# The last expert layer of a four-layer decoder: row scatters replaced by a slot table and gathers

## The reference

```python
group_scores = sg.max(axis=-1)
_, gtop = jax.lax.top_k(group_scores, LG)
keep_g = jnp.sum(jax.nn.one_hot(gtop, G, dtype=jnp.float32), axis=1) > 0
masked = jnp.where(keep_g[:, :, None], sg, -jnp.inf).reshape(-1, E)
_, idx = jax.lax.top_k(masked, K)
...
cap = max(1, int(CAP_FACTOR * N * K / E))
pos = (jnp.cumsum(oh, axis=0) * oh).sum(-1) - 1
keep = pos < cap
...
xe = xp[buf_tok].reshape(E, cap, DIM)
h = jax.nn.silu(jnp.einsum('ecd,edh->ech', xe, w1)) * jnp.einsum('ecd,edh->ech', xe, w3)
out = jnp.einsum('ech,ehd->ecd', h, w2) * buf_w.reshape(E, cap, 1)
y = jnp.zeros((N + 1, DIM), x.dtype).at[buf_tok].add(out.reshape(E * cap, DIM))[:N]
z = jax.nn.silu(xf @ sw1) * (xf @ sw3) @ sw2
return (y + z).reshape(shape)
```

## Time and profile before

| what | us |
|---|---|
| three runs, lowest / median / highest | 3349.03 / 3350.38 / 3354.73 |
| the profiled execution, its own time | 3352.86 |
| its span, first to last instruction | 3351.1 |
| PE busy (86% of the span) | 2880.7 |
| DVE busy (57%) | 1918.6 |
| ACT busy (42%) | 1409.0 |
| POOL busy (18%) | 598.1 |

### The profile page before, as it was taken

One profiled execution on the slowest core, in us unless ns is written; L12 is line 12 of the kernel. 1 busy time (PEld: TensorE's weight loads), 2 busy tenths in 40 slices (PEclk: granted clock), 3 DMA queues, 4 the chain that ended last, 5 costly groups with the idle time before them and its releaser, 6 DMA issues. The chain is left out here.

```text
span 3351.1 us, 46532 instructions
## 1 busy us (share of the span) xinstructions
PE 2880.7 (86%) x13948; PEld 2113.6 (63%) x13949; DVE 1918.6 (57%) x3700; ACT 1409.0 (42%) x2923; POOL 598.1 (18%) x544
## 2 busy tenths in 40 slices
PE   5695789965997989999599999999999997256997
PEld 4684455535885779999366666666666664234664
DVE  4314465405555354444688888888888884442332
ACT  1233534421211224445277676777767775100000
POOL 0122101111331200000201111111111111154554
PEclk9797879986998879999799999999999998587998
DMA  1342000003232010000011000001100000425776
GB/s 39 128 136 82 14 14 14 14 0 110 82 99 88 1 39 26 25 13 1 23 27 24 22 18 19 20 16 29 21 22 20 16 15 3 184 81 160 168 170 136
DMA packets 157228, 177.45 MB, mean 53 GB/s; under 512 B 37664, under 2 KB 130998, under 8 KB 155510
## 3 DMA queue, kind: packets, MB, share of 16 engines
q1 hardware_dynamic: 120150, 116.15, 12.1%
q0 software_dynamic: 20512, 35.54, 4.7%
q10 hardware_dynamic: 16416, 24.12, 2.1%
HBM read 105.77 MB, written 49.18 MB: 46 GB/s over the span
## 5 line engine op out<-in xcount | busy, mean ns | idle before, releaser
L2065 DVE TENSOR_TENSOR l3a_pt_lo<-l3a_pt,l3a_pt_hi 128x512 fp32r<-128x512 f32 (+2 forms) x640 | 463.8, 730 | 96.4 <-ACT l3a_pt L1959 92.1
L1958 ACT ACTIVATE l3a_pt_hi<-l3a_banks 128x512 fp32r<-128x512 f32 (+2 forms) x640 | 382.5, 598 | 322.7 <-PE l3a_banks L1904 258.8
L1959 ACT ACTIVATE l3a_pt<-l3a_banks 128x512 f32<-128x512 f32 (+2 forms) x640 | 378.0, 591 | 0.0
L2039 DVE TENSOR_REDUCE l3a_maxima<-l3a_banks 128x1 f32<-128x1178 f32 x256 | 351.1, 1375 | 1.8 <-PE l3a_banks L1855 0.6
L1904 PE MATMUL l3a_banks<-l3a_pt_hi,l3a_v 128*65 128x512 f32 (+2 forms) x640 | 286.6, 448 | 8.0 <-ACT l3a_out L1973 8.0
L1914 PE MATMUL l3a_banks<-l3a_q,l3a_k 128*128 128x512 f32 (+2 forms) x640 | 257.1, 402 | 7.4 <-DVE l3a_q L2002 4.6
L1915 PE MATMUL l3a_banks<-l3a_q,l3a_k 72*128 72x512 f32 (+5 forms) x640 | 253.8, 397 | 0.0
L1904 PE MATMUL l3a_banks<-l3a_pt_hi,l3a_v_lo 128*65 128x512 f32 (+2 forms) x640 | 252.7, 395 | 0.0
L1904 PE MATMUL l3a_banks<-l3a_pt_lo,l3a_v 128*65 128x512 f32 (+2 forms) x640 | 252.5, 394 | 0.0
L1855 PE MATMUL l3a_banks<-l3a_k,l3a_q 128*128 128x512 f32 (+1 forms) x768 | 213.1, 387 | 18.6 <-DVE l3a_maxima L2039 17.5
L1855 PEld LDWEIGHTS l3a_banks<-l3a_k,l3a_q 128*128 128x128 f32 x768 | 139.6, 192 | 64.0 <-DVE l3a_maxima L2039 41.9
(11 more groups left out here) (563 smaller groups left out, 6065.0 us busy)
## 6 DMA issues: line engine op xcount, KB each, us to landing
l3f_w<-in_L_ffn_w SPq DMA_DIRECT2D x96, 256.0 KB, 3.1
l0f_w<-in_L_ffn_W ACTq DMA_DIRECT2D x12, 1024.0 KB, 6.5
l3f_slots_x<-l3f_empty SPq DMA_DIRECT2D x10, 1168.0 KB, 15.4
l3f_x_rows<-l3f_slots_x SPq DMA_DIRECT2D x32, 292.0 KB, 3.9
l1f_w<-in_L_ffn_W ACTq DMA_DIRECT2D x18, 512.0 KB, 5.2
l2f_w<-in_L_ffn_w SPq DMA_DIRECT2D x16, 512.0 KB, 4.5
l3a_q<-l3a_q SPq DMA_DIRECT2D x64, 128.0 KB, 2.3
l3a_k<-l3a_k SPq DMA_DIRECT2D x64, 128.0 KB, 2.3
```

Source lines behind the costliest of these rows:

```text
L1958: act.activation(a.pt_hi[0:rows, n % a.pt_slots, :], a.st_bank[0:rows, n % 2, :], ACT.Exp, bias=bias, scale=scale)
L1959: act.activation(a.pt[0:rows, n % 4, :], a.st_bank[0:rows, n % 2, :], ACT.Exp, bias=bias, scale=scale).then_inc(a.exped, 1)
L2039: dve.tensor_reduce(a.maxima[:, n:n + 1], banks.rearrange("p a b -> p (a b)")[:, 0:KEYS], AX.X, ALU.max).then_inc(a.maxed, 1)
L2065: dve.tensor_tensor(a.pt_lo[0:rows, slot, :], a.pt[0:rows, n % 4, :], a.pt_hi[0:rows, slot, :].bitcast(F32), ALU.subtract).then_inc(a.lo_m ...
```

## The change

The expert picks use an operation that returns the eight largest values of a row (`max`) and one that replaces given values in a row (`match_replace`), once per tile. A slot number, one over all experts (384 slots each), is split into lane (lowest seven bits) and column (the rest, 96 of them). One-hot rows of column times token number and of lane, multiplied on PE and summed over the 64 (tile, pick) pairs, give a table: lane x column to token. POOL gathers each expert's rows with it from one copy of the rows in DRAM. The shared expert's blocks move in between.

```diff
-            for n in range(CLEARS):
-                rows = slots_x[n * P * CLEAR:(n + 1) * P * CLEAR, :].rearrange("(p n) d -> p (n d)", p=P)
-                sp.dma_start(rows, empty[:].rearrange("p n d -> p (n d)")).then_inc(cleared, 16)
...
+            for q in range(4):
+                sp.dma_start(rows[4 * q * P:4 * (q + 1) * P, :].rearrange("(t p) d -> p t d", p=P), x_ext[:, 4 * q:4 * (q + 1), :]
+                             ).then_inc(rows_kept, 16)
...
-                    load_rows(sp, e + 2, u)
...
-                for t in range(TILES):
-                    pool.indirect_dma_start(slots_x, bass.IndirectOffsetOnAxis(scatter_index[:, k, t:t + 1], 0), x_ext[:, t, :], None
-                                            ).then_inc(scattered, 16)
+            def fetch(u):
+                for j, (at, n) in enumerate(PIECES):
+                    pool.indirect_dma_start(x_rows[0:n, u, j, :], None, rows, bass.IndirectOffsetOnAxis(in_index[0:n, u, j:j + 1], 0)
+                                            ).then_inc(x_loaded[u], 16)
...
+            def run(e, u, more, first=False):
+                if more:
+                    pool.wait_ge(indexed, e + 1)
+                    pool.sem_inc(taken, 1)
+                    fetch(u)
+                if not first:
+                    pool.wait_ge(summed, e * 48)
+                    pool.sem_inc(y_free, 1)
                 pool.wait_ge(meta_kept, e + 1)
                 pool.wait_ge(y_kept, e * 3 + 4)
...
-                pool.wait_ge(summed, e * 48 + 48)
-                pool.sem_inc(y_free, 1)
...
+            shared_hidden(2)
+            for n in range(ENTRIES):
...
+                ins = pe.matmul(p_y[:, 0, 0:TABLE], at_lane[:, n, :], of_token[:, n, :], start=n == 0, stop=n == ENTRIES - 1)
+            ins.then_inc(inverted, 1)
...
+            def take_largest(largest, values, width, left):
+                for t in range(TILES):
+                    ins = dve.max(largest[:, t, :], values[:, t, 0:width])
+                step(ins)
+                step(dve.memset(largest[:, :, K:8], NEVER))
+                for t in range(TILES):
+                    ins = dve.match_replace(left[:, t, :], largest[:, t, :], values[:, t, :], TAKEN)
+                step(ins)
```

More of the change, by code:

```diff
@@ L2823, in run @@
                                             compute_op=ALU.add).then_inc(summed, 16)
-                pool.wait_ge(summed, e * 48 + 48)
-                pool.sem_inc(y_free, 1)
-            experts(pool, run)
+            run(0, 0, True, first=True)
+            run(1, 1, True)
+            with pool.Fori(1, E // 2 - 1) as i:
+                for u in range(2):
+                    run(i * 2 + u, u, True)
+            for u in range(2):
+                run(E - 2 + u, u, False)
         @block.tensor
@@ L2918, in _, with shared_silu @@
             act.copy(probs[:], scores[:]).then_inc(probs_kept, 1)
-            for b in range(4):
+            def shared_silu(b):
                 for f in range(FC):
@@ L2950, in _ @@
             dve.wait_ge(probs_kept, 1)
-            dve.wait_ge(constants, 5)
+            dve.wait_ge(constants, 10)
             step(dve.tensor_scalar(restart[:], restart[:], 0.0, None, ALU.is_gt))
-            step(dve.tensor_reduce(groups[:].rearrange("p t g -> p (t g)"), scores[:].rearrange("p t (g n) -> p (t g) n", g=G), AX.X, ALU.max))
-            for k in range(KEPT_GROUPS):
-                choose(dve, step, groups[:], group_pick[:], group_order[:], total[:], best[:], 2.0)
-            step(dve.tensor_scalar(group_kept[:], groups[:], 0.0, 2.0, ALU.is_ge, ALU.mult))
@@ new lines, in shared_mult, with shared_add @@
+            def shared_mult(b):
+                for f in range(FC):
+                    dve.wait_ge(z_silu_kept, b * FC + f + 1)
+                    if b >= 1:
+                        dve.wait_ge(z_out, 4 * b)
+                    dve.tensor_tensor(z_hidden[:, f, :], z_silu[:, f, :], p_h[:, 2 + f, :], ALU.mult).then_inc(z_kept, 1)
+            def shared_add(b):
+                for t in range(4 * b, 4 * b + 4):
+                    dve.wait_ge(z_out, t + 1)
+                    dve.scalar_tensor_tensor(chip.x[:, t, :], p_xt[:, t % 2, 0:D], chip.gates[:, 7:8], chip.x[:, t, :],
+                                             ALU.mult, ALU.add).then_inc(z_added, 1)
@@ L2966, in _ @@
+            shared_mult(0)
+            take_largest(largest_scores, open_scores, E, left_scores)
+            shared_add(0)
+            step(dve.tensor_scalar(chosen[:], left_scores[:, :, 0:E], TAKEN, None, ALU.is_le))
             dve.sem_inc(chose, 1)
-            step(dve.tensor_reduce(total[:], weight[:].rearrange("p k t -> p t k"), AX.X, ALU.add))
+            step(dve.tensor_reduce(total[:], largest_scores[:, :, 0:K], AX.X, ALU.add))
             step(dve.tensor_scalar(total[:], total[:], 1e-9, None, ALU.add))
@@ L2990, in _ @@
[L2990 to L2999 removed]
+            step(dve.tensor_tensor(scores[:], chosen[:], rank[:].rearrange("p e t -> p t e"), ALU.mult))
@@ new lines, in _ @@
+            for t in range(TILES):
+                ins = dve.max(places[:, t, :], scores[:, t, :])
+            step(ins)
+            step(dve.tensor_scalar(slot[:], places[:, :, 0:K], -1.0, None, ALU.add))
+            step(dve.tensor_scalar(lane[:], slot[:], P - 1, None, ALU.bitwise_and))
+            step(dve.tensor_scalar(column_of[:], slot[:], 7, None, ALU.logical_shift_right))
+            shared_mult(1)
+            flat_lane, flat_column = lane[:].rearrange("p t k -> p (t k)"), column_of[:].rearrange("p t k -> p (t k)")
@@ new lines, in _ @@
+            shared_mult(2)
+            dve.wait_ge(inverted, 1)
+            step(dve.scalar_tensor_tensor(spare[:], p_y[:, 0, 0:TABLE], 0.0, own[:], ALU.is_equal, ALU.mult))
+            step(dve.scalar_tensor_tensor(table[:, 0:TABLE], p_y[:, 0, 0:TABLE], float(TOKENS), spare[:], ALU.add, ALU.add))
+            step(dve.tensor_copy(in_index[:].rearrange("p u j -> p (u j)"), table[:, 0:2 * PIECE_COLUMNS]))
+            dve.sem_inc(tabled, 1)
+            shared_add(2)
+            shared_mult(3)
@@ L3033, in run @@
                     keep_meta(e + 1, 1 - u, e + 2)
+            step(dve.memset(table[:, TABLE:], TOKENS))
             for counted in (xt_kept, h_kept, y_kept):
```

168 lines of the change are left out of this document (87 added, 81 removed).

## The result

The changed kernel takes 3318.7 us (median of four runs, 3316.53 to 3320.95), the kernel before beside it 3349.7. The ratio is 0.9907 (95% interval 0.989 to 0.9925): 31 us faster. The forecast was 3310 us, a gain of 40.

What follows compares the result with a forecast made beforehand. POOL, at 9.13 us per expert against PE's 8.77, would bound the loop. S at 2992, first scatter-add at 3006, then 31 steps of 9.3: last add 40.4 us earlier, 3310 us against 3350.38; range 3297 to 3338.

Steps and rivals of the forecast that it cites:

- The way to S: From the picks to S, the start of PE's first turn of rows: S at 2992 us, before 3043.39.
- Picks: On DVE ahead of the table: group picks 6.3 us, score picks 5.3, with 0.12 per max and 0.20 per replacement.
- The products: 64 products on PE for the table: 0.16 us each, between 0.11 at full clock and 0.22 at half.
- 9.3: Period of the expert loop in us, taken between the ends 9.13 and 10.1; 31 steps make 288.3.
- the forecast case: S near 2992 and a loop period of 9.13 to 9.7 us; chance 0.68.
- POOL's sum: POOL's time per expert in the loop: three scatter-adds, three gathers and six idle gaps of 0.30, 9.13 us.
- Landing + 5.0: Loop through PE: a gather's landing plus 5.0 us is the least period, 7.6 to 10.1, most likely 9.2.
- The adds' landing: Scatter-adds on POOL: the wait for landing has 5.1 us from the last add's start before it holds POOL.
- One sign that the prediction named for being wrong: In the loop: POOL idle before scatter-adds by more than 0.3 us would point to landing or PE's loop.
- Landing as the holder: Rival in the loop: rows landing in 5.1 us make the period 10.1 and the time 3335 us; chance 0.15.
- DVE slowing POOL: Rival in the loop: each gather stretched by 0.72 us, period 11.3, kernel slower at 3372 us; chance 0.07.
- The table: Rival ahead of the loop: slower picks and products put S at 3010, no change, 3350 us; chance 0.05.

Runs made afterwards that it cites:

- one_weights: Changed kernel with only the first two experts' weights loaded and used for all experts: 3304.9 us.
- ahead3: Changed kernel with three buffers of rows instead of two, three experts' rows gathered ahead of the loop, and the loop written out: 3318.1 us.
- deep: Changed kernel with eight buffers of rows, eight experts gathered ahead, no fetch in every fifth step, and the loop written out: 3321.9 us.
- seq_rows: Changed kernel with POOL's gathers replaced by plain loads of 320 consecutive rows per expert on SP: 3291.6 us.
- two_sums: Changed kernel with seven buffers of rows, fewer fetches, and even and odd experts adding into separate arrays merged at the end: 3300.0 us, repeated 3304.5.
- old_picks: Changed kernel with groups and experts picked by the steps of the kernel before instead of eight-largest operations: 3341.5 us.
- pool_fill: Changed kernel with one extra tile fill on POOL, and a wait for it, after the gathers of each of 30 experts: 3356.1 us.

## Why the prediction was right, and where its sums were off

**The way to S** was right as a whole, 2 us short, by terms that cancel. Picks: 4.8 and 4.5 us from groups and scores, priced 6.3 and 5.3, since max and replace lie below the values taken. Adds of block 0: 3.05 for 4.0. Against that, adds of block 1 took 4.8 for 4.0 and block 2's outputs 5.95 for 3.8. The products cost 0.16 each, as taken between the ends; that was luck, for the clock fell amid them. The windows of the changed kernel over block 1's second half, block 2's hidden products, the 64 products and block 2's outputs, and then two that part the levels:

```profile
2946.00:2951.00 5.00, 4.07 (x9) 3.20 (x10) 2.00 (x5) 0.38 (x1) 0.00 (x0) 0.50 0.00 0
2951.00:2958.00 7.00, 7.00 (x17) 3.00 (x15) 7.00 (x7) 3.26 (x7) 0.00 (x0) 0.93 0.00 0
2958.00:2968.00 10.00, 10.00 (x66) 9.88 (x64) 2.40 (x3) 1.97 (x4) 0.00 (x0) 0.71 0.01 2
2968.00:2973.50 5.50, 5.50 (x17) 4.47 (x17) 2.14 (x6) 0.00 (x0) 3.05 (x3) 0.59 0.19 50
...
2952.00:2962.00 10.00, 10.00 (x51) 6.54 (x49) 8.39 (x8) 5.23 (x10) 0.00 (x0) 1.00 0.01 2
2963.00:2972.00 9.00, 9.00 (x34) 8.19 (x35) 1.50 (x5) 0.00 (x0) 1.91 (x2) 0.50 0.04 7
```

Block 1's second half follows 6.28 us without work and has the lower level throughout; from 2952 to 2962 the clock is full, and from 2963 to 2972, over the rest of the products and most of block 2's outputs, it is low again. The durations of the earlier trace rows come from stretches at full clock, which was to be said with them.

**The loop** is where the gain was over-stated, by 12.9 us. The term that was mis-sized is "9.3", measured at 9.715, just above the 9.7 that the forecast case allowed: the loops were the right two, their alternation was priced too low, and the clock was not priced at all.
- POOL's sum, forecast 9.13, measures 9.36: adds 1.62, 1.58, 1.43 and gathers 1.02, 0.97, 0.90, each a little above the rows used. one_weights shows that this is the floor. Over 31 steps 2 us more than 9.3.
- "Landing + 5.0" was the right second loop. Gathers landed in up to 4.5, within, and gave 9.46 to 10.31 in ten steps: 3.7 us.
- Not foreseen: the clock. Five waits of 1.2 to 1.4 us were followed by outputs of 5.1, and these steps, the waits included, cost 9.4 us, more than both terms above.
- The adds' landing "has 5.1 us ... before it can hold POOL": ahead3 shows it at up to 6.0 with 0.9 for the release on top, a third loop of about the same length. In the changed kernel it is hidden.
- One sign that the prediction named for being wrong came: POOL stood idle before scatter-adds by more than 0.3 us in about half of the steps. The time is within its range all the same, since the second loop held only every second step.

**The rivals.** Landing as the holder was given 10.1 in every step and 0.15; it holds every second one. DVE slowing POOL did not happen: the 96 gathers took 0.90 to 1.19, median 0.97, the adds at most 1.65. The table was not late.

## What to carry to other kernels

When two loops over the same queue come out within half a microsecond of each other, forecast the larger and add for their alternation; the mean step here lay above POOL's loop and above the 9.2 taken for the other. Draw every wait on a landing as a loop of its own, also one that is hidden, since a fix of the first (ahead3, deep) only uncovers it; here 8.73 took both landings out of the way and fewer fetches besides. And serial accumulation into one array costs issue plus landing per round; a second array took that off the path here, for a merge of 8.4 us.

## What was not expected of the hardware

- A wait of PE of 1.2 to 1.4 us at full clock was followed by a stretch at a mean of 0.66 to 0.73. In the loops of all runs, behind the first expert, each fall of the clock came after a wait of PE, of 1.12 to 2.41 us, whatever it waited for; in the four runs whose PE had no wait of that length (seq_rows, one_weights and both of two_sums) it never fell. But it is not the length alone: in the changed kernel a wait of 1.60 had no such effect and one of 1.21 had, and old_picks shows none behind waits of up to 2.06. What decides is open. A line of the kernel before and one of ahead3, whose PE waits for DVE:

```profile
3302.64 5.04 PE L2902 MATMUL l3f_p_y<-l3f_w,l3f_hidden 128*128 128x256 f32 x12 [1.69 <-DVE l3f_hidden L3020]
```

```profile
3215.28 5.06 PE L2922 MATMUL l3f_p_y<-l3f_w,l3f_hidden 128*128 128x256 f32 x12 [1.45 <-DVE l3f_hidden L3076]
```

- The clock also fell while PE was shown busy throughout: full from 2952 to 2962 us, low from 2963 to 2972, amid the 64 products and the outputs behind them (windows above).
- A wait of POOL that was not yet met cost 0.6 to 0.8 us on top of what it waited for: 1.08 from the fill's end to the next transfer in pool_fill and 0.93 from the landing in ahead3, against 0.30 without a wait.
- An indexed gather of 64 rows took 0.90 to issue, one of 128 rows 0.97 to 1.02: nearly all of it is per transfer.
